# A hand-laid order of five instruction queues, laid anew, with 78 unread warming products in place of 106

## The reference

```python
mod = (_silu(L0_c) @ L0_wmod).reshape(L0_c.shape[0], 6, 1, -1)
sa, ca, ga, sb, cb, gb = ...
h = _layernorm(x) * (1 + ca) + sa
#   attention block: x' = h + softmax(q k / 4 + bias) v Wo + bo   (16 heads, causal, window 128)
#                    x' + gelu(LN(x') W1 + b1) W2 + b2
x = x + ga * _L0_attn_ref(h, ...)
h = _layernorm(x) * (1 + cb) + sb
#   mixing block:    sigmoid(xr Wr) * (relu(xk Wk)^2 Wv), xr and xk mixed from h and h one token earlier
x = x + gb * _L0_ffn_ref(h, ...)
```

## Time and profile before

| | |
|---|---|
| median of 3 runs | 619.79 us (619.20 to 621.26) |
| the profiled execution | 619.02 us |
| its span, first to last instruction | 617.3 us |
| mean granted TensorE clock | 0.99 |
| PE, ACT, DVE, POOL busy | 91%, 72%, 68%, 61% |
| chain that ended last | PE 54%, DVE 20%, ACT 13%, issue 6%, POOL 4%, DMA 2% |

### The profile page before, as it was taken

One profiled execution on the slowest core, in us unless ns is written; L12 is line 12 of the kernel. 1 busy time (PEld: TensorE's weight loads), 2 busy tenths in 40 slices (PEclk: granted clock), 3 DMA queues, 4 the chain that ended last, 5 costly groups with the idle time before them and its releaser, 6 DMA issues.

```text
span 617.3 us, 16387 instructions
## 1 busy us (share of the span) xinstructions
PE 560.3 (91%) x6448; PEld 436.6 (71%) x6448; DVE 417.1 (68%) x830; ACT 446.9 (72%) x749; POOL 378.1 (61%) x610
## 2 busy tenths in 40 slices
PE   8798987889898998999899989899999999999996
PEld 5467765666766776677667767677777768877785
DVE  4786676794656968786967777757766484465453
ACT  2616676679868787887879686978697798956642
POOL 4277527738947357676776679575748377953330
PEclk9999988989999999999999999999999999999999
DMA  5555435413224034422334152332522134111111
GB/s 163 218 162 129 115 83 161 121 53 81 74 70 111 20 86 123 102 77 71 101 96 116 43 142 88 90 91 74 135 49 69 47 87 122 55 29 36 44 44 34
DMA packets 46363, 55.72 MB, mean 90 GB/s; under 512 B 11643, under 2 KB 33469, under 8 KB 46286
## 3 DMA queue, kind: packets, MB, share of 16 engines
q1 hardware_dynamic: 44454, 53.81, 31.8%
q10 hardware_dynamic: 1832, 0.87, 0.6%
HBM read 22.31 MB, written 4.49 MB: 43 GB/s over the span
## 4 chain that ended last, share of the span: by engine, by line
PE 54%; DVE 20%; ACT 13%; issue 6%; POOL 4%; DMA 2%; ACTq 0%; SPq 0%; DVEq 0%; POOLq 0%
DVE nmax L1853 5%; PE rest L361 4%; PE rest L486 3%; PE quad L398 3%; PE rest L447 3%; PE rest L474 3%; PE rest L498 3%; PE quad L342 3%; PE rest L449 3%; PE rest L448 3%; DVE hid_lo L1914 2%; ACT p L1151 2%; PE quad L307 2%; DVE quad L1850 2%; ACT rest L1202 2%
## 5 line engine op out<-in xcount | busy, mean ns | idle before, releaser
L2588 POOL TENSOR_SCALAR_AFFINE_SELECT p<-p 128x448 f32<-128x448 f32 x64 | 39.0, 610 | 88.1 <-ACT p L1151 63.5
L1853 DVE TENSOR_REDUCE nmax<-quad 128x8 f32<-128x1032 f32 x64 | 78.9, 1233 | 2.2
L430 PE MATMUL rest<-bt_hi,w_hi 128*128 128x256 f16 x256 | 70.2, 274 | 5.0 <-DVE hid_lo L1914 3.5
L1151 ACT ACTIVATE p<-quad,scale_s 128x576 f32<-128x576 f32 (+1 forms) x73 | 59.0, 823 | 20.0 <-PE quad L342 19.7
L1202 ACT ACTIVATE rest<-rest,bias,scale_g 128x256 f32<-128x256 f32 x128 | 62.8, 533 | 12.0 <-PE rest L432 11.5
L447 PE MATMUL rest<-w_hi,hid_hi 128*128 128x256 f16 x256 | 69.9, 273 | 1.7 <-DVE hid_lo L1914 1.7
L432 PE MATMUL rest<-bt_hi,w_lo 128*128 128x256 f16 x256 | 69.8, 273 | 0.0
L431 PE MATMUL rest<-bt_lo,w_hi 128*128 128x256 f16 x256 | 69.8, 273 | 0.0
L449 PE MATMUL rest<-w_hi,hid_lo 128*128 128x256 f16 x256 | 69.8, 272 | 0.0
L448 PE MATMUL rest<-w_lo,hid_hi 128*128 128x256 f16 x256 | 69.8, 272 | 0.0
L1914 DVE SCALAR_TENSOR_TENSOR hid_lo<-rest,inv_f,hid_hi 128x512 f16<-128x512 f32 x64 | 46.5, 740 | 29.1 <-ACT hid_hi L1212 29.1
(11 more groups left out here) (239 smaller groups left out, 1544.4 us busy)
## 6 DMA issues: line engine op xcount, KB each, us to landing
k_st<-k_two SPq DMA_DIRECT2D x64, 128.0 KB, 2.5
v_blk<-vn SPq DMA_DIRECT2D x16, 512.0 KB, 6.0
q_st<-q_two SPq DMA_DIRECT2D x64, 64.0 KB, 2.2
k_st<-k_two SPq DMA_DIRECT2D x64, 64.0 KB, 2.0
rb<-den_rows SPq DMA_DIRECT2D x16, 256.0 KB
x<-x SPq DMA_DIRECT2D x16, 256.0 KB, 3.0
out<-x SPq DMA_DIRECT2D x16, 256.0 KB, 2.2
xa<-x SPq DMA_DIRECT2D x7, 512.0 KB, 4.3
```

The lines of the kernel that those rows point to most:

```text
L430: e.matmul(dst, w1_hi[:, k, ms], bt_hi[:, k, :], start=(k == 0), stop=False)
L1151: e.activation(p32[gp % SLOTS][:, c0:c0 + 2 * w].rearrange("p (n c) -> p n c", n=2), (rest if gp < APART else quad)[:, b0 % HQ:b0 % HQ + 2 ...
L1853: e.tensor_reduce(nmax[:, :, :, qt].rearrange("p a j -> p j a"), quad[:, :, 2 * QB - 2:2 * WIN].rearrange("p j (c a) -> p j a c", a=2), AX ...
```

## The change

No operation on data is added or taken away. The lists of all five engines are written in another order, and `warm` is called with other numbers: 78 products in 17 calls for 106 in 24. The most and the largest moves lie in the first 140 us; behind that, pairs of neighbouring calls change places on PE, ACT and DVE, and POOL's list is reordered over longer stretches. `warm` also waits in another way: calls with n from 20 to 24 for `s_peak` (met long before), calls with n of 25 or more for the first twelve groups' exponentials.

```diff
-                if n == WARM:
-                    e.wait_ge(s_peak, 10)
-                if n == WARM + 5:
-                    e.wait_ge(s_ex, 2 * APART)
+                if WARM <= n < WARM + 5:
+                    hold(e, s_peak, 10)
+                if n >= WARM + 5:
+                    hold(e, s_ex, 2 * APART)
...
             maxima(3, 3)
-            warm(24, 2)
             scores(11, 2, 4)
+            warm(29, 6)
             max_rows(3)
...
             exps(5, 0, 2)
+            setup_w1()
+            copy_den(0)
             exps(5, 2, 4)
...
             low_m(1)
+            setup_s1()
+            stats_x(2)
             low_qk(2)
             maxima(2, 0)
-            stats_x(2)
             maxima(2, 1)
```

More of the change, by code:

```diff
@@ L611, in _ @@
             scores(0, 0, 2)
+            setup_mod_cols(0, 0)
+            maxima(1, 0)
+            setup_mod_cols(0, 1)
+            setup_mod_cols(1, 0)
+            scores(0, 2, 4)
             setup_mod_cols(1, 1)
[L613 to L616, removed]
+            warm(12, 2)
             maxima(1, 1)
+            setup_f1()
+            warm(14, 2)
+            warm(15, 1)
             scores(1, 0, 2)
+            maxima(1, 2)
             scores(1, 2, 4)
-            maxima(1, 2)
-            warm(15, 6)
+            warm(16, 4)
             maxima(1, 3)
-            setup_f1()
-            warm(16, 1)
             scores(2, 0, 2)
@@ L694, in _ @@
             warm(30, 7)
-            warm(31, 2)
             scores(13, 0, 2)
+            scores(13, 2, 4)
+            transposes_b(1)
+            scores(14, 0, 2)
             values(2, 0)
-            scores(13, 2, 4)
-            scores(14, 0, 2)
+            max_rows(4)
             scores(14, 2, 4)
-            transposes_b(1)
-            max_rows(4)
+            warm(35, 3)
             scores(15, 0, 2)
-            values(2, 1)
             scores(15, 2, 4)
             up(0, 3, 4)
+            values(2, 1)
             project(5)
@@ L2234, in _ @@
             low_b(2)
+            stats_x(4)
             residual_b(1)
-            stats_x(4)
             maxima(6, 1)
+            divide(4)
             gated(0)
@@ L2288, in _ @@
             maxima(8, 2)
-            mix(3)
+            scale_x(5)
             low_f(4, 2, 3)
             low_f(4, 3, 4)
-            scale_x(5)
+            mix(3)
+            scale_c(6)
             maxima(8, 3)
+            output(2)
+            low_b(5)
+            low_m(8)
             shift_x(5)
-            scale_c(6)
-            low_m(8)
-            output(2)
             low_qk(9)
-            low_b(5)
-            divide(7)
             stats_h(5)
             add_y(4)
+            divide(7)
             gated(3)
@@ L2330, in _ @@
             stats_b(7)
-            divide(8)
             gated(4)
             maxima(10, 2)
-            mix(5)
             low_f(6, 2, 3)
             low_f(6, 3, 4)
-            output(4)
+            mix(5)
+            scale_c(8)
             maxima(10, 3)
@@ L2340, in _ @@
             low_m(10)
-            scale_c(8)
             low_qk(11)
+            low_b(7)
+            output(4)
+            divide(9)
             shift_x(6)
-            low_b(7)
-            divide(9)
+            add_y(6)
             stats_h(6)
             gated(5)
-            add_y(6)
             maxima(11, 0)
@@ L2373, in _ @@
             residual_a(9)
-            divide(10)
             stats_b(9)
             low_f(8, 1, 2)
+            scale_c(10)
             gated(6)
             maxima(12, 2)
+            stats_x(7)
+            mix(7)
             low_f(8, 2, 3)
+            low_f(8, 3, 4)
+            maxima(12, 3)
             output(6)
-            low_f(8, 3, 4)
-            mix(7)
-            maxima(12, 3)
-            scale_c(10)
+            low_m(12)
             scale_x(7)
-            low_m(12)
             low_qk(13)
@@ L2707, in _ @@
             rstd_x(1)
-            bias_h(0)
             modulate_x()
             rstd_h(1)
+            setup_gates()
             select(0)
-            setup_gates()
+            setup_f1()
             select(1)
+            bias_h(0)
             select(2)
```

597 lines of the change are left out of this document (292 added, 305 removed).

## The result

The changed kernel took 611.92 us (median of 4 runs, 611.63 to 612.85), the kernel before 619.81 us: ratio 0.9878, 95% interval 0.9856 to 0.99, 7.9 us less. The profiled execution took 611.74 us around a span of 609.9, so spans are compared as times are. An execution more than 1.5% above the fastest of its kernel is called slow here, and the ratios leave it out.

What follows compares the result with a forecast made beforehand. It took PE, busy 560.3 of 617.3 us, as the bound, with room mainly in the first 139 us. Terms 0 - 0.6 - 1.1 - 0.3 + 0.2 + 0.5 - 0.7 - 0.6 - 1.0 + 0.3 = -3.3 gave 616.5 us from 619.8; range 612.5 to 620.5.

Steps and rivals of the forecast that it cites:

- `setup_attn`, +0.3: 0 to 49 us: three additions stand before the normalisation that the first transposes wait for, costing 0.3 us.
- 49 to 61, -0.6: Unit 1's last maxima: setup_modt and setup_f1 leave, removing DVE's 0.60 us wait; -0.6, between 0 and -1.2.
- 61 to 73, -1.1: stats_x(2) moves from between two maxima into DVE's wait for project(2); -1.1, ends -1.65 and 0.
- 73 to 95, -0.1: context(0) loses group 5's second scores ahead of it, -0.3; a gate-row load delays scale_c(0)'s last DMA, +0.2.
- The rival of the low parts: Weights' products on DVE meet POOL's work, 1.0 us longer each, four of them, half at PE: 618.2; chance 0.12.
- 95 to 107, +0.5: warm(29, 6) before max_rows(3) makes PE wait for group 11's exponentials; +0.5, ends 0 and +0.9.
- "Sum 0" for 0 to 49 us: Opening up to 49 us: small losses and sooner first scores cancel; 0, from -0.8 to +0.6.
- 107 to 139 us, -0.7: low_f(0, 1, 2) goes ahead of setup_w2 and scale_x(3), removing PE's 1.27 us wait; -0.7, between 0 and -1.3.
- 139 us to the end, -1.0: PE's 1.11 us wait at keys(6) shrinks as POOL's additions move away, other stops unchanged; -1.0, ends -3 and +1.5.
- The clock, -0.6: First 139 us: half of the first two half-clock stretches vanish, 0.6 us each; -0.6, ends +1.8 and -5.1.
- The rival of the clock: First 139 us: fewer fillers bring more half-clock stretches, 1.7 us each; four extra give 623.3; chance 0.10.
- The rival "much more": No half-clock stretch comes and the middle loses as many waits as swaps could give: 612.8; chance 0.17.

Runs made afterwards that it cites:

- a_ref_b: The changed kernel again, unedited, timed beside a_keep_b on one chip: 614.23 us, ratio 0.9896.
- b_stats: Kernel before with stats_x(2) moved ahead of low_qk(2) on DVE and 5 instead of 11 warming products between group 4's scores: 622.59 us, ratio 1.0058.
- b_gates_stats: b_stats with setup_gates also moved ahead of select(0) on GpSimd: 620.0 us, ratio 1.0008.
- a_no29: Changed kernel without the call of six warming products, warm(29, 6), ahead of max_rows(3): 613.66 us, ratio 0.991.
- b_lowf: Kernel before with low_f(0, 1, 2) moved ahead of setup_w2 and scale_x(3) on DVE: 618.72 us, ratio 0.9999.
- h2_rest: Kernel before up to the first maxima of unit 5, then the changed lists: 616.81 us, ratio 0.9968.
- a_nofill: Changed kernel with only the first call's 9 warming products instead of 78: 622.32 us, ratio 1.0049.
- a_keep_b: Changed kernel with 111 warming products instead of 78, second timing, beside the reference on one chip: 613.67 us, ratio 0.9915.
- h_first: Changed lists up to the last maxima of unit 1 (about 56 us), then those of before: 621.05 us, ratio 1.0.
- h_mid: Kernel before with the changed lists only from project(4) to the first maxima of unit 5: 617.01 us, ratio 0.9939.

## Why the prediction was right or wrong

Right, by its own steps:

- *`setup_attn`, +0.3.* With no half clock between (`a_ref_b`), `setup_mod` to `maxima(0, 0)` takes 19.53 us against 19.33: +0.2. W2's earlier load cost nothing beyond that, as said.
- *49 to 61, -0.6.* -0.54 from `maxima(1, 0)` to `transposes_a(1)`, the same in four traces.
- *61 to 73, -1.1.* -1.44 from `project(2)` to `context(0)`. The reason was half a reason: it named the statistics and took the load for late by little. By `b_stats` and `b_gates_stats` the statistics need the earlier gates on GpSimd, and the two together give 0.7 of the 1.4.
- *73 to 95, -0.1.* -0.08, with 3.4 us of half clock in the kernel before alone, so the agreement is partly luck. `scale_c(0)` still waits for its DMAs, and PE stands 0.81 us ahead of `context(1)`, as expected. W1's low part takes 3.45 us for 2.47 and is hidden, as is W2's with 3.40: its first half waits behind an addition on POOL (1.92 us for 1.27), its second runs beside selects (1.60 for 1.28). The rival of the low parts had the price right (1.0 each) and the cover wrong. DVE in the changed kernel:

```profile
77.25 3.45 DVE L1991 SCALAR_TENSOR_TENSOR w_lo<-stage,col,w_hi 128x1024 f16<-128x1024 f32 x2
...
83.33 0.69 DVE L1867 TENSOR_TENSOR ct<-rest,rb 128x512 f32<-128x512 f32 x1 [0.73 <-DMA rb<-den_rows]
...
130.75 3.40 DVE L1899 SCALAR_TENSOR_TENSOR w_lo<-stage,inv_f,w_hi 128x1024 f16<-128x1024 f32 x2
```

- *95 to 107, +0.5.* +0.63, by `a_no29`.

Wrong:

**1. "Sum 0" for 0 to 49 us.** The starts say -1.80 - 1.25 = -3.05 us from `maxima(0, 0)` to `maxima(1, 0)`, without any half clock on either side; with the +0.2 ahead of it -2.85, against ends of -0.8 and +0.6. This is the step that failed, and three parts of it were wrong. First the low k of unit 0. DVE and POOL in the kernel before:

```profile
29.53 2.48 DVE L1840 SCALAR_TENSOR_TENSOR k_two<-kc,pick,k_two 128x512 f16<-128x512 f32 x2 [0.38 <-ACT kc L1118]
...
36.62 0.42 DVE L1850 COPY_PREDICATED quad<-later,quad 128x248 f32<-128x248 int16 x1 [0.81 <-PE quad L307]
```
```profile
29.86 1.57 POOL L2616 TENSOR_TENSOR h<-h,row_b 128x512 f32<-128x512 f32 x1
```

And in the changed kernel:

```profile
30.35 1.47 DVE L1834 SCALAR_TENSOR_TENSOR k_two<-kc,pick,k_two 128x512 f16<-128x512 f32 x2 [1.59 <-ACT kc L1112]
...
36.13 0.42 DVE L1844 COPY_PREDICATED quad<-later,quad 128x248 f32<-128x248 int16 x1 [0.52 <-PE quad L307]
```
```profile
29.61 5.52 POOL L2524 TENSOR_SCALAR h<-xa,mv_x,rs_x 128x256 f32<-128x256 f32 x4
```

`bias_h(0)`, an addition of two tensors on POOL, lay beside the low k; the change moves it away and the two products take 1.47 us instead of 2.48: -1.0 on the chain from the low k to the maxima. It is the second product that waited: it took 1.79 to 1.80 us in all eight traces with the old start and 0.77 to 0.78 in all twelve with the new one. The Trainium skill (SBUF — State Buffer, Who interferes with whom) counts any GpSimd instruction that reads SBUF; here POOL's modulation, with one tensor read, ran beside the same DVE instruction and cost it nothing. One tensor read is not a rule either: POOL's selects read one, and W1's second half took 1.60 us beside them for 1.28. The prediction had the sign of this term wrong. It feared that `setup_exp` would go up beside POOL's modulation and grow (+0.3), but it had been beside it before and left it:

```profile
40.49 1.27 DVE L2075 TENSOR_TENSOR scale_s<-inv_s 128x1 f32<-128x1 f32 x1
```
```profile
25.98 0.15 DVE L2069 TENSOR_TENSOR scale_s<-inv_s 128x1 f32<-128x1 f32 x1
```

Second, the warming calls of 9 and 8 products were too long: DVE waited 0.81 and 0.58 us for PE and now 0.52 each time, -0.35. Two more between `max_rows(0)` and `project(1)`, where nothing waited, cost 0.45. The sentence on which the prediction rested, that such a product fills a wait and does not make one, was false in this place.

Third, from 38.4 to 47.9 us PE had 0.12 us of idle time in all, and there three calls of `setup_mod_cols`, of about 0.4 us each, stood ahead of `values(0, 0)`; moved behind the scores they give their whole length, -1.25. The prediction knew of them, but held that ACT's copies of v "are no sooner than that". `maxima(1, 0)` does begin right behind the last copy, by 0.05 us in both traces. But the copies follow PE's value products and came sooner with them. ACT before and now:

```profile
47.99 0.66 ACT L1130 ACTIVATE vn<-quad 128x256 f32<-128x256 f32 x2 [0.50 <-PE quad L287]
```
```profile
45.20 1.22 ACT L1124 ACTIVATE vn<-quad 128x256 f32<-128x256 f32 x4
```

The three sizes are read from traces; no run moved one of these calls alone.

**2. 107 to 139 us, -0.7.** Without half clock on either side it is 31.55 us (`b_stats`) to 29.27: -2.3 of order, and the stretch at half clock in the kernel before had added only 0.2. Of these 31.55 us PE was idle 5.18, of the 29.27 only 2.99. The named move gives nothing alone (`b_lowf`): behind the 1.27 us stood another 1.26, for `low_m(4)`, which the rows of before did not show because half clock had covered them. ACT's exponentials, which the prediction put next, were not it.

**3. 139 us to the end, -1.0.** -2.4, within its own ends of -3 and +1.5; `h2_rest` confirms it. From `project(5)` to `down(15, 1)` seven traces with the old lists have a median of 455.7 us and ten with the new ones 452.8, -2.9. It was mis-sized because one wait was looked up and the others were taken as unchanged.

**4. The clock, -0.6.** The changed kernel spends more time at half clock, not less: medians of 9.9 us before and 16 over its own executions. At 0.3 us each that is about +2. The rival of the clock had the sign, not the size: it asked for a loss against before, and the order's gain was larger. That fillers do hold the clock is shown by `a_nofill`, 9.5 us. That these 28 would have been worth keeping is not shown: in `a_keep_b` 33 more, in other places, gained nothing clear.

Compared at a mean clock of 0.992 and more, the order is worth 618.9 - 610.6 = 8.3 us, though only three executions of the changed kernel are among these (610.3 to 612.9); the prediction's sum without its clock term was 2.7. The parts above add up to 0.2 - 3.05 - 0.7 - 1.4 - 0.1 + 0.6 - 2.3 - 2.4 = -9.2; where the other microsecond goes is open. The rival "much more" came near the time with 612.8, but by luck: it asked for no stretch at half clock, and three came. The forecast's mark "idle time grows by about 4 to 5" failed too: idle time stayed as it was, since fillers were dropped where they held PE up.

## What to carry to other kernels

Before pricing a stretch by the waits that end in it, ask where the bounding engine has none: there each instruction moved out counts in full, and a filler laid a little too long makes the next engine wait. Ask too what a wait behind the one that you remove would be: it can be hidden in the trace you read, as `low_m(4)`'s was. A move on one engine is worth what its partners on the other queues let it be, so price the set and not its members; `b_stats` lost 3.4 us with a move that belongs to a gain. And where the clock moves the time by more than the effect, compare starts of the same calls between traces without half-clock stretches before believing a median.

## What the runs showed of the hardware

- One program on one chip took 617.1 to 624.7 us (19 executions of the kernel before beside `a_ref_b`), and 617.0 to 624.7 over 112 on five chips, in step with the mean granted clock (0.981 to 0.997). Which stretches fall to 1.2 GHz differs between executions of the same lists.
- DVE beside POOL: the second low part of k took 1.79 us behind POOL's addition and 0.78 beside its modulation.
- A fall can last: in `h_first` and `a_ref_b` PE was busy 13.1 of 13.7 us, much of it on products of few columns, and stayed at half clock for four times the length of a single stretch. In the 3.4 us before, in `h_first`, it had been busy for 3.30 on such products too, at a granted clock of 1.00. Why it stays down was not tried.
- At the start the granted clock reads 1.00 while the same four products take 3.75 us in one execution and 1.96 in another: there the granted clock does not show the rate.
- A stretch of 3.4 us at half clock cost 0.2 us where a wait of PE stood behind it (31.78 against 31.55 us).
- Twice, in `h_mid` and `a_keep_b`, the last `out_project` came 1.3 to 1.6 us late behind a denominators' DMA, with lists that in other executions did not wait there. It stayed open why.
